# One attention stage of a four-layer block: mask addition and row maximum in one VectorE instruction per head instead of two over eight heads

## The chip, the cores and the metric

The kernel runs on one NeuronCore of a Trainium2 chip. The metric is the device time of one execution in microseconds, the median of several runs. The core has five engines with a queue each: PE (TensorE), DVE (VectorE), ACT (ScalarE), POOL (GpSimd) and SP (SyncE, which only issues DMAs). Each takes its instructions strictly in order; engines wait for each other by semaphores alone.

## The reference, cut to what matters

A stack of four gated layers over x of shape (16, 128, 256): in each, an attention block and a feed-forward block, each fed by a layer norm and added back with a tanh gate. The change is in the attention of layer 1, which has 32 heads of 8 elements:

```python
q, k, v = split_heads(h @ Wq), split_heads(h @ Wk), split_heads(h @ Wv)      # (16, 32, 128, 8), then rope on q and k
scores = einsum('bhqd,bhkd->bhqk', q, k) * inv_sqrt_d
scores = scores + attention_mask                                            # (16, 1, 128, 128), 0 or -1e9
scores = maximum(scores, finfo(float32).min)
w = softmax(scores, axis=-1)
attn = einsum('bhqk,bhkd->bhqd', w, v)
a_scores = tanh(gate) * softmax(einsum('bhqd,bhkd->bhqk', q, a_k) * inv_sqrt_d)  # second key set, from the context
attn = attn + einsum('bhqk,bhkd->bhqd', a_scores, a_v)
return attn @ Wo
```

## The kernel before, in words

Everything is written as queues by hand: for each engine a function lists its instructions, and marks (semaphores that count up) tie the queues together. `mark.at(n)` is the n-th increment of a mark.

The layer 1 attention works on 64 steps: step n is batch row b = n // 4 and the eight heads 8 * (n % 4) to 8 * (n % 4) + 7. All scores of a step are a 128 x 1024 tile in PSUM, 128 columns to a head. There are two score tiles with one buffer each: `self_bank` (banks 2 and 3) for the layer's own keys, `adapter_bank` (banks 4 and 5) for the keys from the context. For the own keys a step goes:

- PE, `pe_scores` (L1743): eight matmuls fill `self_bank`. For step n it first waits for `mask_used.at(n)`, the sign that step n - 1 has been read out of the bank.
- DVE, `dve_self_scores` (L1878 to L1888): one `tensor_tensor` over all 1024 columns adds the mask (broadcast over the heads) and writes the sum to `d_t[n % 3]` in SBUF (L1886, signals `mask_used`), then one `tensor_reduce` takes the maximum of each head, negated, into the eight columns of `max_t[n % 3]` (L1888, signals `maxed`). It waits for the sum by semaphore.
- The shift by the maximum is split: ACT, `act_shift` (L2003), does heads 0 to 3 with four activations (Identity with a bias per row), POOL, `pool_shift` (L2083), heads 4 to 7 with one `tensor_tensor`. Both wait for `maxed`.
- PE, `pe_turn` (L1764), transposes the eight 128 x 128 tiles into `turn_bank`, ACT exponentiates them (`act_exp`, L2011, two halves), PE, `pe_weigh` (L1789), multiplies with the values; DVE, `dve_normalise` (L1902 to L1907), reads the result, takes the reciprocal of the sums and scales, every second step; POOL, `pool_sums` (L2065), adds the two attentions.

For the context's keys `dve_adapter_max` (L1895) takes the negated maximum, which goes by a transposition on PE (`pe_turn_top`, L1732), ACT (L1986, L1987, L1991), POOL (`pool_rest_top` L2088, `pool_lo_top` L2092) and a DMA into the rows that `pe_adapter_turned` (L1775) reads.

The order is that of the loops over u in `pe_program`, `dve_program`, `act_program` and `pool_program`. At u DVE takes `dve_adapter_max(u + 5)`, then `dve_self_scores(u + 2)`, then a slot for the projections of a later pair of rows, `dve_turn_back` (L1914) and `dve_normalise(u - 1)`. PE takes `pe_turn(u)`, `pe_weigh(u - 1)`, `pe_adapter_turned(u)`, a projection slot, `pe_adapter_scores(u + 6)` (L1755) and `pe_scores(u + 3)`. ACT takes the exponents of u, and between its halves `act_shift(u + 1)`; POOL `pool_shift(u + 1)`, a slot, and `pool_sums` in every second step. Every eight steps (a pair of rows) the slots also hold the projections and rotations of a later pair: PE L1694, L1708, L1724, L1726 and L1797, DVE L1857 and L1859, ACT L1955 to L1978, POOL L2052, L2056, L2069, L2070 and L2078.

Of the kernel before, what the change touches and what calls it, by code (L numbers as in the profile page):

```python
# [11 lines left out]
ALU = mybir.AluOpType  # L12
ACT = mybir.ActivationFunctionType
AXX = mybir.AxisListType.X

P = 128
NB = 16
S = 128
# [9 lines left out]
LOWEST = -3.38e38  # L28
# [71 lines left out]
def split_cols(ap, k):  # L100
    return ap.rearrange("p (k n) -> p k n", k=k)
# [1499 lines left out]
def l1_attention(m):  # L1601
    nc, A = m.nc, m.A
    pe, dve, act, pool, sp = nc.tensor, nc.vector, nc.scalar, nc.gpsimd, nc.sync
# [8 lines left out]
    mask_t = [mem.f32(S) for _ in range(2)]  # L1612
    max_t = [mem.f32(8) for _ in range(3)]
# [4 lines left out]
    d_t = [mem.f32(8 * P) for _ in range(3)]  # L1618
# [21 lines left out]
    mask_ready, mask_used = m.mark("mask_ready"), m.mark("mask_used")  # L1640
# [9 lines left out]
    scored, maxed, shifted = m.mark("scored"), m.mark("maxed"), m.mark("diff_by_act")  # L1650
    shifted_pool = m.mark("sel_loaded")
# [17 lines left out]
    self_bank, adapter_bank = m.bank(2, 2), m.bank(4, 2)  # L1669
# [207 lines left out]

    def dve_self_scores(n):  # L1878
        b = n // 4
        d3, s3, mx = split_cols(d_t[n % 3], 8), split_cols(self_bank, 8), max_t[n % 3]  # L1880
        dve.wait_ge(*scored.at(n + 1))
        if n >= 3:
            dve.wait_ge(*turned.at(4 * (n - 3) + 2))
        if n % 4 == 0:
            dve.wait_ge(*mask_ready.at(b + 1))
        dve.tensor_tensor(d3, s3, mask_t[b % 2].unsqueeze(1).broadcast_to([P, 8, S]), ALU.add).then_inc(*mask_used.up())  # L1886
        dve.wait_ge(*mask_used.at(n + 1))
        dve.tensor_reduce(mx, d3, AXX, ALU.max, negate=True).then_inc(*maxed.up())  # L1888

    def dve_adapter_max(n):  # L1890
        b, s = divmod(n, 4)
# [39 lines left out]
    def dve_program():  # L1931
        dve.wait_ge(*m.x_l0f.at(NBLK))
        dve_norm_stats(1)
        dve.wait_ge(*v_cleared.now())
        for u in range(FIRST, LAST):
            if 0 <= u + AHEAD < NS:
                dve_adapter_max(u + AHEAD)
            if 0 <= u + 2 < NS:
                dve_self_scores(u + 2)
            dve_pro_slot(2 * u)  # L1940
            if u >= 3 and u % 2 and u <= NS + 1:
                dve_turn_back((u - 3) // 2)
            if 1 <= u <= NS:
                dve_normalise(u - 1)
            dve_pro_slot(2 * u + 1)
            dve_ffn_norms(u)
        dve_ffn_apply(7)
# [51 lines left out]
    def act_shift(n):  # L1999
        act.wait_ge(*maxed.at(n + 1))  # L2000
        for j in range(4):
            d = d_t[n % 3][:, j * P:(j + 1) * P]
            last = act.activation(d, d, ACT.Identity, bias=max_t[n % 3][:, j:j + 1])  # L2003
        last.then_inc(*shifted.up())

    def act_exp(i):
# [28 lines left out]
    def act_program():  # L2035
        act.wait_ge(*m.x_l0f.at(NBLK))
        act.wait_ge(*v_cleared.now())
        for u in range(FIRST, LAST):
            if 0 <= u < NS:
                act_exp(2 * u)  # L2040
            act_pro_slot(2 * u)
            if 0 <= u + 1 < NS:
                act_shift(u + 1)
            if 0 <= u < NS:
                act_exp(2 * u + 1)
            act_pro_slot(2 * u + 1)
# [32 lines left out]

    def pool_shift(n):  # L2080
        d3, mx = split_cols(d_t[n % 3][:, BANK:2 * BANK], 4), max_t[n % 3][:, 4:8]
        pool.wait_ge(*maxed.at(n + 1))
        pool.tensor_tensor(d3, d3, mx.unsqueeze(2).broadcast_to([P, 4, S]), ALU.add).then_inc(*shifted_pool.up())  # L2083

    def pool_rest_top(b):
        pool.wait_ge(*top_hi.at(b + 1))
# [45 lines left out]
    def pool_program():  # L2132
        pool.wait_ge(*m.x_l0f.at(NBLK))
        pool_roots(1)
        for kind in "aq":
            pool_clear_stack(kind, 2)
        for u in range(FIRST, LAST):
            if 0 <= u + 1 < NS:
                pool_shift(u + 1)
            pool_pro_slot(2 * u)  # L2140
            if 1 <= u <= NS and u % 2 == 0:
                pool_sums(u // 2 - 1)
            pool_pro_slot(2 * u + 1)
            for n in FFN_NORMS.get(u - NS, ()):
                ln_root(m, n, f_var, f_rstd)
# [2374 lines left out]
```

## Time and profile before

| | |
|---|---|
| median of 3 runs | 1979.42 us (1979.06 to 1988.81) |
| the profiled execution | 1980.39 us, of which the span of the program's instructions 1979.1 us |
| busy in the span | PE 87%, DVE 69%, ACT 48%, POOL 40% |
| mean granted clock of TensorE | 0.95 of full |
| first and last own-score sum (L1886) of the changed stage | 625.3 and 976.8 us |

The busy shares are means over all eight blocks. The changed stage lies between about 610 and 990 us, a fifth of the span; what a change in it is worth is read from the queues in that stretch. In the rows below a line of the timeline gives the start from the span's start, the length, the engine, the line of the kernel, the operation, what it writes and reads, its shape and how many were merged. The time from one start to the next on one engine is called the pitch here; it is shorter than the length where two instructions overlap.

### The profile page before, as it was taken

How to read it: one execution, taken by the hardware profiler on the slowest of the kernel's cores; microseconds unless marked ns; L12 is line 12 of the kernel's file. 1: busy time of each engine (PE TensorE's matmuls, PEld its weight loads, DVE VectorE, ACT ScalarE, POOL GpSimd, SP SyncE). 2: the span in 40 equal slices, each digit the busy share in tenths (PEclk: the TensorE clock that was granted, in tenths of full speed). 3: DMA queues.
4: the chain of work that ended last, by engine and by line, in shares of the span. 5: the costliest groups of instructions: out<-in, count | busy, mean ns of one | idle time of the engine just before them, and what ended most of it. 6: DMA issues, size and time to landing. Idle time of an engine off the chain costs nothing.

```text
span 1979.1 us, 35080 instructions
## 1 busy us (share of the span) xinstructions
PE 1716.5 (87%) x12221; PEld 1181.1 (60%) x12221; DVE 1370.8 (69%) x3299; ACT 942.1 (48%) x2227; POOL 789.6 (40%) x957
## 2 busy tenths in 40 slices
PE   6888888959897888888888787777999999987998
PEld 2444444636665777777666555455777777766445
DVE  8888873613357898988836889874576676666446
ACT  2666663203323676767735456433444444443352
POOL 3333321264654555655334555211124334433340
PEclk7999999979997999999989799789999999999899
DMA  4444422046863344334023453108200000030767
GB/s 108 104 120 102 94 55 79 31 161 225 298 178 84 79 86 85 78 78 89 16 82 96 120 148 87 42 1 275 78 18 36 32 8 4 13 96 13 232 214 305
DMA packets 180430, 200.35 MB, mean 101 GB/s; under 512 B 86500, under 2 KB 150129, under 8 KB 176928
## 3 DMA queue, kind: packets, MB, share of 16 engines
q1 hardware_dynamic: 161920, 155.92, 28.9%
q0 software_dynamic: 15168, 41.54, 6.1%
q8 instruction: 99, 1.62, 0.4%
q10 hardware_dynamic: 3168, 0.66, 0.2%
q14 instruction: 75, 0.61, 0.1%
HBM read 131.88 MB, written 75.44 MB: 105 GB/s over the span
## 4 chain that ended last, share of the span: by engine, by line
PE 49%; DVE 23%; ACT 8%; issue 8%; POOL 4%; DMA 3%; another core or an unknown queue 2%; ACTq 1%; SPq 1%; DVEq 0%; POOLq 0%
PE psum L3464 3%; PE psum L1052 3%; PE psum L3390 3%; PE psum L389 3%; PE psum L1329 2%; DVE sbuf L539 2%; PE psum L3439 2%; PE psum L352 2%; PE psum L3457 2%; PE psum L2276 2%; ACT sbuf L3827 2%; PE psum L1348 2%; PE psum L1064 2%; PE psum L4047 1%
## 5 line engine op out<-in xcount | busy, mean ns | idle before, releaser
L539 DVE TENSOR_REDUCE sbuf<-psum 128x2 f32<-128x512 f32 x256 | 164.9, 686 | 34.2 <-PE psum L352 33.2
L190 POOL TENSOR_TENSOR sbuf<-sbuf 128x1 f32<-128x1 f32 x128 | 73.2, 574 | 271.8 <-DVE sbuf L182 271.5
L2011 ACT ACTIVATE sbuf<-psum 128x512 f32<-128x512 f32 x256 | 138.6, 594 | 73.8 <-PE psum L1764 69.1
L3827 ACT ACTIVATE sbuf<-psum,sbuf 128x128 f32<-128x128 f32 x256 | 113.6, 456 | 89.0 <-DVE sbuf L3639 88.8
L681 ACT ACTIVATE sbuf<-psum 128x1024 f32<-128x1024 f32 x128 | 130.4, 1020 | 37.2 <-PE psum L374 29.7
L3919 POOL DMA_INDIRECT l_slot_inputs<-sbuf x96 | 97.2, 1013 | 100.7 <-DVE sbuf L3710 75.7
L3464 PE MATMUL psum<-sbuf 128*128 128x256 f32 x512 | 123.8, 385 | 4.9 <-DVE sbuf L3657 4.9
L3390 PE MATMUL psum<-sbuf 128*128 128x256 f32 x512 | 117.0, 382 | 0.8 <-ACT sbuf L3791 0.8
L352 PE MATMUL psum<-sbuf 112*128 112x256 bf16 x512 | 104.1, 288 | 12.8 <-DVE sbuf L539 7.7
L3390 PEld LDWEIGHTS psum<-sbuf 128*128 128x128 f32 x512 | 97.0, 192 | 20.6 <-issue 8.6
L3464 PEld LDWEIGHTS psum<-sbuf 128*128 128x128 f32 x512 | 93.5, 193 | 16.1 <-issue 5.8
L352 PEld LDWEIGHTS psum<-sbuf 112*128 112x128 bf16 x512 | 41.6, 101 | 91.2 <-DVE sbuf L539 52.9
L1895 DVE TENSOR_REDUCE sbuf<-psum 128x8 f32<-128x1024 f32 x64 | 77.5, 1211 | 26.2 <-PE psum L1755 26.2
L1052 PE MATMUL psum<-sbuf 128*128 128x512 f32 (+1 forms) x192 | 88.0, 602 | 0.0
L2003 ACT ACTIVATE sbuf<-sbuf 128x128 f32<-128x128 f32 x256 | 81.5, 398 | 0.0
L3597 DVE COPY sbuf<-psum 128x1024 f32<-128x1024 f32 x32 | 39.2, 1224 | 60.2 <-ACT sbuf L3798 40.1
L1888 DVE TENSOR_REDUCE sbuf<-sbuf 128x8 f32<-128x1024 f32 x64 | 78.1, 1220 | 2.2
L3835 ACT ACTIVATE sbuf<-psum 128x512 f32<-128x512 f32 x64 | 38.4, 600 | 85.0 <-PE psum L3447 84.6
L374 PE MATMUL psum<-sbuf 128*128 128x512 bf16 x256 | 78.1, 387 | 0.3 <-ACT sbuf L681 0.2
L1886 DVE TENSOR_TENSOR sbuf<-psum,sbuf 128x1024 f32<-128x1024 f32 x64 | 77.6, 1213 | 1.1 <-PE psum L1743 1.1
L1789 PE MATMUL psum<-sbuf 128*16 128x128 f32 x2048 | 70.5, 280 | 8.2 <-DVE sbuf L1902 6.9
L1764 PE MATMUL psum<-sbuf 128*128 128x128 f32 x512 | 71.7, 284 | 6.7 <-ACT sbuf L2011 6.6
(436 smaller groups left out, 4507.7 us busy)
## 6 DMA issues: line engine op xcount, KB each, us to landing
l_pair_outputs<-sbuf SPq DMA_DIRECT2D x24, 512.0 KB, 7.1
sbuf<-in_l_gu_pairs SPq DMA_DIRECT2D x32, 384.0 KB, 8.4
sbuf<-l_pair_outputs SPq DMA_DIRECT2D x16, 768.0 KB, 16.0
sbuf<-l_q_parts SPq DMA_DIRECT2D x16, 384.0 KB
l_q_parts<-sbuf SPq DMA_DIRECT2D x64, 96.0 KB, 2.3
sbuf<-l_q_parts SPq DMA_DIRECT2D x32, 192.0 KB
l_k_parts<-sbuf SPq DMA_DIRECT2D x64, 96.0 KB, 2.2
sbuf<-l_k_parts SPq DMA_DIRECT2D x32, 192.0 KB
```

Source lines behind the costliest of these rows:

```text
L352: last = pe.matmul(score_bank[v % 2][:, j * T0:(j + 1) * T0], q3[0:STACK + 48, h, c * P:(c + 1) * P], k3[0:STACK + 48, h // 4, :], start=T ...
L374: last = pe.matmul(shift_bank[u % 2][:, j * BANK:(j + 1) * BANK], k3[:, g, kc * P:(kc + 1) * P], q_stack[b % 3][:, lo:lo + BANK], start=Tr ...
L539: dve.tensor_reduce(top3[:, 2 * hp:2 * hp + 2, c], score_bank[v % 2].rearrange("p (j t) -> p j t", j=2), AXX, ALU.max, negate=True).then_i ...
L681: act.activation(e_t[u % 12], shift_bank[u % 2], ACT.Exp).then_inc(*exped.up())
L1052: last = pe.matmul(up_bank[v % 2][0:M, n * BANK:(n + 1) * BANK], wn[:, k, fs], xt_t[blk][:, k, :], start=(k == 0), stop=(k == KD - 1))
L1888: dve.tensor_reduce(mx, d3, AXX, ALU.max, negate=True).then_inc(*maxed.up())
L2003: last = act.activation(d, d, ACT.Identity, bias=max_t[n % 3][:, j:j + 1])
L2011: act.activation(e_t[i % 4][:, h * BANK:(h + 1) * BANK], turn_bank[:, h * BANK:(h + 1) * BANK], ACT.Exp).then_inc(*exped.up())
L3390: last = pe.matmul(q_bank[:, j * N:(j + 1) * N], w.wq[:, k, (4 * g + j) * P:(4 * g + j + 1) * P], xt_t[pair % 2][:, k, :], start=(k == 0), ...
L3464: last = pe.matmul(out_bank[:, 0:D], o_t[b % 2][:, h * P:(h + 1) * P], w.wo[:, h, :], start=(h == 0), stop=(h == H3 - 1))
L3827: last = act.activation(e_t[u % 3][:, j * P:(j + 1) * P], score_bank[:, j * P:(j + 1) * P], ACT.Exp, bias=mt[:, j:j + 1], scale=rq[:, lo + ...
L3919: pool.indirect_dma_start(out=route.x_slots[:, :], out_offset=bass.IndirectOffsetOnAxis(ap=route.slot[b][:, k:k + 1], axis=0), in_=xr_t[b ...
```

## The change

One fused instruction per head (`tensor_tensor_reduce`) replaces the sum over eight heads and the maximum over eight heads. It reads 128 columns of `self_bank` and the 128 x 128 mask, writes -(score + mask) to `d_t`, and the minimum of what it wrote, which is the negated maximum, to one column of `max_t`. The two shifts take the turned sign: ACT scales by -1 before it adds the bias, POOL subtracts the tile from the broadcast bias. The two marks change their meaning: `maxed` is now signalled after head 3, for ACT, and `mask_used` after head 7, for POOL and for `pe_scores`. One semaphore wait inside `dve_self_scores` is gone.

```diff
     def dve_self_scores(n):
         b = n // 4
-        d3, s3, mx = split_cols(d_t[n % 3], 8), split_cols(self_bank, 8), max_t[n % 3]
+        mask, mx = mask_t[b % 2], max_t[n % 3]
         dve.wait_ge(*scored.at(n + 1))
         if n >= 3:
             dve.wait_ge(*turned.at(4 * (n - 3) + 2))
         if n % 4 == 0:
             dve.wait_ge(*mask_ready.at(b + 1))
-        dve.tensor_tensor(d3, s3, mask_t[b % 2].unsqueeze(1).broadcast_to([P, 8, S]), ALU.add).then_inc(*mask_used.up())
-        dve.wait_ge(*mask_used.at(n + 1))
-        dve.tensor_reduce(mx, d3, AXX, ALU.max, negate=True).then_inc(*maxed.up())
+        for h in range(2):
+            for j in range(4 * h, 4 * h + 4):
+                head = slice(j * P, (j + 1) * P)
+                last = dve.tensor_tensor_reduce(d_t[n % 3][:, head], self_bank[:, head], mask, -1.0, -LOWEST, ALU.add, ALU.min, mx[:, j:j + 1])
+            last.then_inc(*(maxed, mask_used)[h].up())
...
     def act_shift(n):
-            last = act.activation(d, d, ACT.Identity, bias=max_t[n % 3][:, j:j + 1])
+            last = act.activation(d, d, ACT.Identity, bias=max_t[n % 3][:, j:j + 1], scale=-1.0)
...
     def pool_shift(n):
         d3, mx = split_cols(d_t[n % 3][:, BANK:2 * BANK], 4), max_t[n % 3][:, 4:8]
-        pool.wait_ge(*maxed.at(n + 1))
-        pool.tensor_tensor(d3, d3, mx.unsqueeze(2).broadcast_to([P, 4, S]), ALU.add).then_inc(*shifted_pool.up())
+        pool.wait_ge(*mask_used.at(n + 1))
+        pool.tensor_tensor(d3, mx.unsqueeze(2).broadcast_to([P, 4, S]), d3, ALU.subtract).then_inc(*shifted_pool.up())
```

## Rows read from the trace of the kernel before

**Rows 1.** Busy time by stretch: window, us, then each engine, clock, DMA.
```profile
core 0: us, PE busy (x) PEld busy (x) DVE busy (x) ACT busy (x) POOL busy (x), PEclk, DMA share, GB/s
650.00:950.00 300.00, 258.94 (x3623) 217.25 (x3621) 265.19 (x354) 209.12 (x525) 171.78 (x240) 0.98 0.38 82
```
**Rows 2.** Groups by line, of DVE: count | busy us, mean ns | idle before.
```profile
L1888 DVE TENSOR_REDUCE sbuf<-sbuf 128x8 f32<-128x1024 f32 x64 | 78.1, 1220 | 2.2
L1886 DVE TENSOR_TENSOR sbuf<-psum,sbuf 128x1024 f32<-128x1024 f32 x64 | 77.6, 1213 | 1.1 <-PE psum L1743 1.1
L1859 DVE TENSOR_TENSOR sbuf<-psum,sbuf 128x256 f32<-128x256 f32 x32 | 11.9, 415 | 0.0
L567 DVE TENSOR_TENSOR sbuf<-psum,sbuf 128x64 f32<-128x64 f32 x64 | 11.4, 220 | 1.1
```
**Rows 3.** Waits, 650 to 950 us: total us, times, longest us.
```profile
DVE sbuf L1895 <- PE psum L1755: 16.5, 15, 2.3
DVE sbuf L1902 <- PE psum L1789: 10.6, 9, 1.2
PE psum L1743 <- DVE sbuf L1886: 0.5, 1, 0.5
POOL sbuf L2065 <- DVE sbuf L1907: 75.1, 26, 7.1
```
**Rows 4.** Timeline of DVE, one and a half steps.
```profile
830.02 1.21 DVE L1886 TENSOR_TENSOR sbuf<-psum,sbuf 128x1024 f32<-128x1024 f32 x1
831.26 1.22 DVE L1888 TENSOR_REDUCE sbuf<-sbuf 128x8 f32<-128x1024 f32 x1
832.40 0.42 DVE L178 BATCH_NORM_STATS2 sbuf<-sbuf 128x6 f32<-128x256 f32 x1
...
833.07 0.15 DVE L182 TENSOR_SCALAR sbuf<-sbuf 128x1 f32<-128x1 f32 x1
833.14 0.42 DVE L178 BATCH_NORM_STATS2 sbuf<-sbuf 128x6 f32<-128x256 f32 x1
```
**Rows 5.** The chain that ended last, 829 to 852 us: start, us, what.
```profile
832.40 3.08 issue
835.48 0.02 POOLq L2087
...
837.78 1.26 ACT sbuf L2003 x4
...
849.71 1.80 PE psum L1694 x8
```
**Rows 6.** Timeline of DVE: short instructions without a wait between them.
```profile
61.29 0.36 DVE L567 TENSOR_TENSOR sbuf<-psum,sbuf 128x64 f32<-128x64 f32 x2
852.14 0.75 DVE L1859 TENSOR_TENSOR sbuf<-psum,sbuf 128x256 f32<-128x256 f32 x2
456.58 0.14 DVE L1385 COPY sbuf<-sbuf 128x1 f32<-128x1 f32 x1
456.64 0.14 DVE L1386 TENSOR_SCALAR sbuf<-sbuf 128x1 uint32<-128x1 f32 x1
```
**Rows 7.** Timeline of DVE: short instructions that wait for the one before.
```profile
382.86 0.29 DVE L1151 TENSOR_TENSOR sbuf<-sbuf 128x128 f32<-128x128 f32 x1
383.19 0.29 DVE L1153 TENSOR_REDUCE sbuf<-sbuf 128x8 f32<-128x128 f32 x1
```
**Rows 8.** Timeline of all engines around one step.
```profile
826.95 1.22 DVE L1888 TENSOR_REDUCE sbuf<-sbuf 128x8 f32<-128x1024 f32 x1
830.67 1.04 POOL L2083 TENSOR_TENSOR sbuf<-sbuf 128x512 f32<-128x512 f32 x1
830.67 1.28 ACT L2003 ACTIVATE sbuf<-sbuf 128x128 f32<-128x128 f32 x4
831.68 0.61 PE L1743 MATMUL psum<-sbuf 96*128 96x128 bf16 x8
832.58 1.12 PE L1764 MATMUL psum<-sbuf 128*128 128x128 f32 x8 [0.29 <-ACT sbuf L2011]
834.73 1.07 PE L1789 MATMUL psum<-sbuf 128*16 128x128 f32 x32 [1.03 <-DVE sbuf L1902]
835.51 0.59 POOL L2065 TENSOR_TENSOR sbuf<-sbuf 128x64 f32<-128x64 f32 x2 [3.11 <-DVE sbuf L1907]
```
**Rows 9.** Timeline of DVE at the stage's end.
```profile
964.73 1.21 DVE L1886 TENSOR_TENSOR sbuf<-psum,sbuf 128x1024 f32<-128x1024 f32 x1
968.58 1.22 DVE L1886 TENSOR_TENSOR sbuf<-psum,sbuf 128x1024 f32<-128x1024 f32 x1
971.79 1.18 DVE L1886 TENSOR_TENSOR sbuf<-psum,sbuf 128x1024 f32<-128x1024 f32 x1
```
**Rows 10.** All instructions of one line, whom they wait for, who waits for them.
```profile
L2083 POOL TENSOR_TENSOR sbuf<-sbuf x64: 1027/1036/1052, 629.9 to 983.3; 128x512 f32<-128x512 f32 x64
DVE sbuf L1888: 5.7, 4
```

## The prediction

> **What bounds the kernel now.** I read the groups by line first, to place the changed instructions: 64 sums and 64 maxima of 1.21 to 1.22 us each, 156 us of DVE in all, between 625 and 978 us [rows 2]. Then the busy time of that stretch alone: in 300 us from 650 us, DVE is busy 265.2 us (88%), PE 258.9 (86%), ACT 209 and POOL 172 [rows 1]. No engine but DVE and PE comes near its limit, and the two are close. The waits tell which of them leads. DVE stands still for PE some 27 us in these 300 (16.5 us before L1895, 10.6 us before L1902), while PE waits for the bank that DVE reads only once, 0.5 us [rows 3]. POOL waits 75 us for DVE's L1907, and what stands behind it in POOL's queue waits too. The chain of waits shows what that is worth: from 832.40 to 835.48 it has 3.08 us of "issue" on POOL [rows 5], and the timeline gives that gap its owner, `pool_sums` waiting 3.11 us for DVE L1907 [rows 8], behind which stand the small POOL steps that ACT and then PE wait for. So the piece is a DVE stretch in disguise, and one that starts with the two instructions of the change at 830.02 [rows 4]. After it the chain goes over ACT and PE [rows 5] for some 16 us, in which DVE, though full, is not what ends last. At the stage's end the sums follow each other by 3.85 and 3.21 us with DVE full in between [rows 9]: there every nanosecond of DVE counts.
>
> A step takes (976.8 - 625.3) / 63 = 5.58 us on average (first and last L1886 start). DVE's idle share, 34.8 us in 300, is 0.65 us of each step.
>
> **What the change removes.** The two instructions take, from the start of the sum to the start of the next instruction, 832.40 - 830.02 = 2.38 us [rows 4]. The second waits for the first, so its start is 1.24 us behind, a little more than the first's length; the next one, with no such wait, starts 1.14 us behind.
>
> **What it adds.** Eight instructions of 128 columns, one input in PSUM and one in SBUF. None like it is in the trace, so I build its cost from its relatives. Two sums of 256 columns from PSUM and SBUF take 0.75 us together, where one takes 0.415: the pitch is 0.33 us [rows 2, 6]. Two of 64 columns take 0.36 us, one of them 0.22: a pitch of 0.14 us [rows 2, 6]. The line through both is 1.0 ns per column, and gives 0.205 us at 128 columns. Then the minimum must be written out, one value per row. I take it as an instruction of its own, as small as the 128x1 ones of L1385 and L182: those start 0.06 to 0.07 us apart when nothing is waited for [rows 4, 6]. I take 0.065, so 0.27 us a head and 8 x 0.27 = 2.16 us a step: 0.22 us less than now. The even point is 2.38 / 8 = 0.298 us a head.
>
> The bounds: if the write-out were free, a head costs 0.205 and a step 1.64 us, 0.74 us less. If the write-out had to wait until the main instruction is through, the main's pitch is that of dependent instructions of this size, 383.19 - 382.86 = 0.33 us [rows 7], and with 0.065 a head costs 0.395, a step 3.16 us, 0.78 us more. I take the value near the middle because the rows without a wait are the nearer relatives: there is no semaphore between the eight instructions.
>
> The Trainium skill bears on this at two places. "Vector Engine (DVE) Microarchitecture Reference", section Measured stream behaviour on trn2, says that an instruction costs about 75 ns beyond its columns once the queue overlaps, programs of several micro-operations included. That would be 8 x (133 + 75) + 8 x 76 = 2.27 us for sixteen instructions, an estimate, and a saving of 0.11 us a step; the rows here are a little below it. Against the change speaks "VectorE: DVE Perf Modes", section on the TRN2 errata: a fixed price of 120 cycles for an instruction that reads PSUM and 58 for one that reads SBUF, and its advice is to have few, large instructions. By it the step would cost about 8 x 258 + 8 x 61 = 2.55 us, an estimate, 0.17 us more than now. The pitch of 0.33 us at 256 columns leaves 0.06 us of fixed price for a PSUM source [rows 6], so the trace disagrees with the larger figure.
>
> **What moves beside it.** `self_bank` was free 1.21 us after a step's start on DVE, now after all eight, 2.16 us: 0.95 us later. In rows 8, PE's L1743 starts at 831.68, and the sum that frees the bank ended at 831.23; it would now be free at about 832.2, 0.5 us later than PE took it. Behind it in PE's queue is L1764, which had 0.29 us of idle before it, and then L1789, which waited 1.03 us for DVE [rows 8]; the delay ends there. Price nothing, and if that cover were gone 0.5 us in perhaps three of eight steps, 64 x 3/8 x 0.5 = 12 us. ACT may start its shift after head 3, 1.1 us into the step instead of 2.4. But its four activations at 830.67 use the maximum of the step before, which ended at 828.17, 2.5 us earlier [rows 8]: ACT is held by its own queue, so nothing is gained. POOL waited for the maximum 4 times, 5.7 us in all [rows 10], and gets it 0.2 us sooner. The turned operands cost no more: the same shapes on both engines. The 128x512 shift on POOL stays at 1.04 us [rows 10]; I put both at zero with 0.1 us a step as a bound either way, since ACT and POOL are 70% and 57% busy [rows 1] and would hide it.
>
> **The sum.** 64 x 0.22 = 14 us less on DVE. Not all comes out: of the eight steps of a pair, the chain runs over two to four on DVE, the rest over ACT, POOL and PE; DVE's other time already has 0.65 us of idle a step, which would only grow. At the two ends of the stage nearly all comes out. I take half: 7 us. From the profiled execution's 1980.39 us that is 1973.4; the execution was 1.0 us above the median of 1979.42, so the forecast is 1972.4 us, 0.35% less.
>
> **Rivals.** (a) The write-out is hidden and the gain comes through. At 0.235 us a head a step saves 0.50 us, 32 us over the stage; half to two thirds is 16 to 21 us: 1958 to 1963 us. For it: the write-out reads no tensor, so the gap that rows 6 show between two instructions may shrink; DVE is the fullest engine. Against it: PE is 86% busy and would lead soon. Anything of over 0.27 us a step at a realised half gives more than 0.5%. (b) It gets slower, by one mechanism: main instruction and write-out do not overlap, at `dve_self_scores`, each head paying a pipeline's drain. From 0.298 us a head on DVE loses. At 0.395 a step is 0.78 us longer, 50 us over the stage; the idle 0.65 us a step takes up perhaps 0.3 of it, which leaves 30 us: 2010 us. At a milder 0.33 us a head it is 0.26 us, and 8 to 16 us: 1988 to 1995. For it: rows 7, and an instruction of a kind the trace doesn't hold. Against it: no row has an unforced drain. (c) The later release of the bank makes PE late and eats the gain: half of the 12 us above against the 7 gained, 1978 us. Against it: PE waited for this bank once in 300 us, and two waits stand behind it as cover. (d) The fused instruction might leave maximum or sum to be done twice: the diff shows neither remains, I give it nothing.
>
> **How the numbers follow.** The forecast 0.42, (a) 0.27, (b) 0.20, (c) 0.11. The range from 1958 to 1990 us holds the forecast and (c), most of (a) and the mild end of (b), and leaves out the serial case and a free write-out that comes through fully (1948 at two thirds of 47 us). 0.5% is 9.9 us, about what a measurement here can tell from no change. The forecast's own spread (0.25 to 0.29 us a head) reaches from 1967 to 1978, so a third of it counts as faster: 0.27 + 0.13 = 0.40 for faster; 0.40 for within 0.5% with (c) and the rest; 0.20 for slower.
>
> **What would show it.** The group of the fused instruction: 512 of them, with a mean of about 0.29 us and a pitch of head to head of 0.27 us with its write-out; if the pitch is above 0.30, (b). PE's wait before L1743 for DVE should appear in a few more steps by a few tenths; if it sums to over 10 us, (c). DVE's busy time in 650 to 950 us should fall and its waits for PE rise from 27 us; L2003 and L2083 should keep their durations. The forecast is wrong if the last score instruction of the stage doesn't start about 7 us sooner, or if the time changes outside 610 to 1000 us.

## The result

| | before | after |
|---|---|---|
| median, same chip, 5 runs each | 1982.45 us (1979.06 to 1988.81) | 1964.88 us (1964.35 to 1976.86) |
| ratio, 95% interval | | 0.9918 (0.9895 to 0.9941) |
| DVE for one step's scores, first start to next instruction | 2.38 us | 1.68 us |
| first to last start of PE's scores L1743 | 623.2 to 976.6 us | 622.9 to 961.4 us |

0.8% faster, 16 us, in the range forecast (1958 to 1990 us) and some 7 us below the forecast value. The forecast started from 1979.42 us, the median of three of the five runs of before in this table, so the ratio is the fairer comparison: 0.35% less was forecast, 0.8% less was measured.

The gain shows in the stage. In both kernels the first scores start at 623 us; the last start is 15.2 us sooner after the change, where the forecast had about 7:

```profile
L1743 PE MATMUL psum<-sbuf x512: 216/219/314, 622.9 to 961.4; 96*128 96x128 bf16 x171
```

(All instructions of a line: shortest/median/longest ns, then first and last start.) The profiled execution of the changed kernel took 1976.86 us all the same, the longest of its five. It lost the rest outside the changed stage: from the end of the stage's last PE matmul (L1797, 978.4 us) to the end it needed 997 us, where the trace of before needed 985. Another execution of the same program (`after_again`) needed 986 us, and the other kernels below between 981 and 992. That scatter belongs to the stages behind, which are the same code, and it goes with the clock granted to TensorE in them: 0.93 of full in those 997 us, 0.94 in the 985 us of before, 0.95 in the 986 us of `after_again`.

The same holds between whole executions. Beside `after_again` the kernel before ran 34 times, from 1983.55 us at a mean granted clock of 0.952 to 1999.67 us at 0.940. Over the runs of that series a clock lower by 0.01 goes with 11 to 13 us more (an estimate, by lines fitted to the recorded times and clocks). The gain itself is not the clock: the mean is 0.947 in the 34 runs of before and 0.947 in the 11 of the changed kernel.

### The profile page after: what moved, and what is told of

Read it like the earlier page. It is cut to its first block, busy times and chain, and to the rows that moved or that the text cites. A ratio compares the mean times of both kernels' runs of the same rounds, so it can differ in the third digit from the quotient of the medians.

```text
span 1975.5 us, 35976 instructions
## 1 busy us (share of the span) xinstructions
PE 1726.9 (87%) x12221; PEld 1186.7 (60%) x12221; DVE 1330.4 (67%) x4195; ACT 942.1 (48%) x2227; POOL 790.8 (40%) x957
## 4 chain that ended last, share of the span: by engine, by line
PE 51%; DVE 20%; ACT 10%; issue 7%; POOL 4%; DMA 3%; another core or an unknown queue 2%; ACTq 1%; SPq 1%; DVEq 0%; POOLq 0%
PE psum L3392 3%; PE psum L1052 3%; PE psum L389 3%; PE psum L3466 3%; PE psum L1329 2%; DVE sbuf L539 2%; PE psum L3441 2%; PE psum L352 2%; ACT sbuf L3829 2%; PE psum L3459 2%; PE psum L2278 2%; PE psum L1348 2%; PE psum L1064 2%; PE psum L1764 1%
## 5 line engine op out<-in xcount | busy, mean ns | idle before, releaser
L1889 DVE CUSTOM_DVE_ANT_0 sbuf<-psum,sbuf 128x128 f32<-128x128 f32 x512 | 112.5, 284 | 0.5 <-PE psum L1743 0.5
L3392 PEld LDWEIGHTS psum<-sbuf 128*128 128x128 f32 x512 | 98.7, 195 | 21.5 <-issue 8.8
L3466 PEld LDWEIGHTS psum<-sbuf 128*128 128x128 f32 x512 | 93.6, 193 | 16.1 <-issue 5.8
L2005 ACT ACTIVATE sbuf<-sbuf 128x128 f32<-128x128 f32 x256 | 81.4, 398 | 0.0
L3459 PE MATMUL psum<-sbuf 128*128 128x512 f32 x128 | 69.3, 623 | 9.8 <-ACT sbuf L3837 9.8
L3441 PEld LDWEIGHTS psum<-sbuf 128*128 128x128 f32 x512 | 65.8, 195 | 17.3 <-issue 15.1
L1764 PE MATMUL psum<-sbuf 128*128 128x128 f32 x512 | 70.5, 281 | 5.2 <-ACT sbuf L2013 5.0
```

The source lines that it names most:

```text
L1889: last = dve.tensor_tensor_reduce(d_t[n % 3][:, head], self_bank[:, head], mask, -1.0, -LOWEST, ALU.add, ALU.min, mx[:, j:j + 1])
L3392: last = pe.matmul(q_bank[:, j * N:(j + 1) * N], w.wq[:, k, (4 * g + j) * P:(4 * g + j + 1) * P], xt_t[pair % 2][:, k, :], start=(k == 0), ...
L3441: last = pe.matmul(score_bank[:, j * P:(j + 1) * P], q[:, 4 * g + j, i * P:(i + 1) * P], kT_t[b % 3][:, g * P:(g + 1) * P], start=True, st ...
L3459: pe.matmul(av_bank, v_t[b % 3][:, g * P:(g + 1) * P], eT_t[u % 2], start=True, stop=True).then_inc(*valued.up())
L3466: last = pe.matmul(out_bank[:, 0:D], o_t[b % 2][:, h * P:(h + 1) * P], w.wo[:, h, :], start=(h == 0), stop=(h == H3 - 1))
```

## The profile after

One head of the fused form is two instructions, as the timeline of DVE shows (start, us, engine, line):

```profile
828.59 0.28 DVE L1889 CUSTOM_DVE_ANT_0 sbuf<-psum,sbuf 128x128 f32<-128x128 f32 x1
828.80 0.08 DVE L1889 DVE_READ_ACCUMULATOR2_ANT sbuf<- 128x1 f32 x1
828.80 0.28 DVE L1889 CUSTOM_DVE_ANT_0 sbuf<-psum,sbuf 128x128 f32<-128x128 f32 x1
829.01 0.08 DVE L1889 DVE_READ_ACCUMULATOR2_ANT sbuf<- 128x1 f32 x1
829.01 0.30 DVE L1916 STREAM_TRANSPOSE sbuf<-sbuf 128x128 f32<-128x128 f32 x1
```

A head starts 0.21 us after the head before, and the read of the accumulator starts at the same 10 ns as the next head: it stands in the list, but not in the pitch. Eight heads take 1.68 us, so DVE saves 0.70 us a step, 45 us over the stage. The groups by line answer to [rows 2]:

```profile
L1889 DVE CUSTOM_DVE_ANT_0 sbuf<-psum,sbuf 128x128 f32<-128x128 f32 x512 | 112.5, 284 | 0.5 <-PE psum L1743 0.5
L1889 DVE DVE_READ_ACCUMULATOR2_ANT sbuf<- 128x1 f32 x512 | 42.2, 82 | 0.0
```

Busy time in the same 300 us as in [rows 1], from 650 to 950 us:

```profile
650.00:950.00 300.00, 269.08 (x3820) 227.61 (x3818) 241.56 (x1128) 219.78 (x554) 176.28 (x246) 0.98 0.38 81
```

PE rises from 86 to 90% and ACT from 70 to 73%: their work is unchanged and passes in less time; DVE falls from 88 to 81%, though it too passes more steps. The waits, which answer to [rows 3]:

```profile
DVE sbuf L1904 <- PE psum L1789: 23.2, 14, 2.6
DVE sbuf L1897 <- PE psum L1755: 22.7, 16, 3.9
DVE sbuf L1857 <- PE psum L1694: 9.4, 12, 1.5
```

DVE now waits for PE 55 us of 300 where it waited 31 (27 and a few at L1857). PE's wait for the score bank (L1743 for DVE) is under no row of that window; over the whole stage it is 2.6 us in 4 places, where before it was 3.4 us in 7. The chain that ended last, in the stretch that answers to [rows 5], has no fused instruction in it; DVE is on it only with the rotation (L1857, L1859):

```profile
824.62 1.70 issue
...
828.63 1.26 ACT sbuf L2005 x4
829.89 0.95 ACT sbuf L2013 x2
830.84 0.49 ACT sbuf L1957
831.33 0.04 issue
831.37 1.13 PE psum L1724 x4
832.50 0.86 PE psum L1726 x4
...
837.78 1.12 PE psum L1764 x8
838.90 1.00 PE psum L1789 x32
839.89 0.67 PE psum L1775 x8
840.56 1.80 PE psum L1694 x8
842.36 0.02 issue
842.38 0.53 DVE sbuf L1857
```

Before, the same chain had 3.08 us of disguised DVE time there ("issue", while POOL waited for DVE's L1907); now that piece is 1.70 us, in which POOL's L2067 waits 1.73 us for DVE's L1909. From ACT's shift to DVE's L1857 it is ACT and PE in turns, 13.75 us in both kernels (837.78 to 851.53 before, 828.63 to 842.38 after).

## The experiments

Each kernel ran against the kernel before on the same chip; the ratio is to it. The interval of a ratio reaches about 3 to 6 us to either side, and a length of the stage is that of one profiled execution at one granted clock. Theory A: the gain is DVE's shorter step, and as much of it comes out as DVE leads. Theory B: it comes from the early signal after head 3 and the wait that is gone.

**The changed kernel again** (no edit).

> The changed kernel once more, as the yardstick of this chip. Theory A (VectorE's shorter step is the whole gain: 1.69 us for the eight heads instead of 2.38, 44 us over 64 steps, of which about a third comes out): a ratio of 0.992 to the kernel before, some 1965 to 1967 us, and again a stage that ends 15 to 16 us sooner. Theory B (the gain is mostly that ScalarE may shift after head 3 and that one wait is gone): the same number here.

Measured: 0.9935 (0.9915 to 0.9956); last scores at 958.4 us, 18 us sooner than before. The result repeats in another series of runs, in which the kernel before took 1990.75 us.

**DVE's time given back.** Behind the fused instructions:

```diff
             last.then_inc(*(maxed, mask_used)[h].up())
+        if n:
+            dve.wait_ge(*padded.at(n))
+        dve.tensor_reduce(idle_t[:, 0:2], m.ident.unsqueeze(1).broadcast_to([P, 2, P]), AXX, ALU.max).then_inc(*padded.up())
```

> The changed kernel, with one idle VectorE maximum over 128x256 of a constant behind the eight fused instructions of each step: about 0.33 us more VectorE time a step (21 us in all), nothing else changed, the signals of the step not delayed. Theory A: half of VectorE's saving is gone, and the time rises by 4 to 9 us over the changed kernel, to 1969 to 1975. Theory B: no change, within 2 us of the changed kernel.

> The same with 128x640: about 0.73 us more VectorE time a step, so that a step costs VectorE as much as before the change (2.4 us) while ScalarE still gets its maxima early and the bank is free 0.5 us later than before. Theory A: back to the time of the kernel before, ratio 0.997 to 1.003. Theory B: stays below, at a ratio of 0.992 to 0.995.

> The changed kernel with an idle maximum over 128x384 behind each step's fused instructions: a VectorE step of about 2.15 us, between the 2.015 us that cost nothing (ratio 0.9927 against 0.9935) and the 2.415 us that cost the whole gain (0.9995). Theory A2 (there is a knee: up to about 2.0 us a step another loop sets the pace, above it over half of each VectorE microsecond comes out): ratio 0.995 to 0.997. Rival A1 (a straight line from 1.69 us on, the flat part being scatter): 0.9965 to 0.998 as well at this point, so the profile has to tell: A2 expects VectorE's waits for TensorE's L1755 and L1789 below 35 us in 650 to 950 us, and the stage some 5 us longer than with 128x256.

Measured, with DVE's time for a step as the traces have it, the waits of DVE for PE (three lines as above) in 650 to 950 us, the length of the stage from the first start of the scores to their last, and the clock granted in that stretch:

| DVE's step | kernel | ratio, 95% interval | DVE waits for PE | stage | clock |
|---|---|---|---|---|---|
| 1.68 us | changed | 0.9918 (0.9895 to 0.9941) | 55.3 us | 338.5 us | 0.97 |
| 1.68 us | changed, again | 0.9935 (0.9915 to 0.9956) | 52.7 us | 334.5 us | 0.98 |
| 2.015 us | idle 128x256 | 0.9927 (0.9901 to 0.9952) | 42.0 us | 343.1 us | 0.98 |
| 2.15 us | idle 128x384 | 0.9952 (0.9934 to 0.9969) | 38.1 us | 348.1 us | 0.98 |
| 2.415 us | idle 128x640 | 0.9995 (0.9976 to 1.0014) | 30.1 us | 357.1 us | 0.97 |
| 2.385 us | before | 1 | 30.6 us | 353.4 us | 0.97 |

The largest dose decides. With DVE's old time the whole gain is gone, to within about 4 us, though the early signal, the missing wait, the new bank release and the turned signs are all still there: theory B falls, theory A stands.

How the gain is spread is less sharp. By its ratio alone the first dose cost nothing, as theory B had it, and the point at 2.15 us came out as the knee theory (A2) had it: ratio 0.9952, 33.2 us of waits at L1755 and L1789, a stage 5 us longer than with 128x256. But a straight line fits the ratios within their intervals as well, and the stage in the traces rises through the first dose too, by 5 to 9 us. The runs' clocks can account for the flat piece: the twelve runs with 128x256 had a mean granted clock of 0.951, the kernel before and the changed one beside them 0.947. Compared at equal clock, by the line through the runs (an estimate, good to about 2 us each; it leaves aside that a kernel may itself shift the clock), the gain is 14 us for the changed kernel, 10 with 128x256, 6 with 128x384 and none with 128x640. That is about a third of the DVE time throughout. A flat stretch or a knee is not shown.

**The sum by head, the maximum over all.**

```diff
-        dve.tensor_tensor(d3, s3, mask_t[b % 2].unsqueeze(1).broadcast_to([P, 8, S]), ALU.add).then_inc(*mask_used.up())
+        for j in range(8):
+            head = slice(j * P, (j + 1) * P)
+            last = dve.tensor_tensor(d_t[n % 3][:, head], self_bank[:, head], mask_t[b % 2], ALU.add)
+        last.then_inc(*mask_used.up())
```

> The kernel before, with its one sum over 1024 columns cut into eight sums of 128 columns; the maximum stays one instruction over 1024. Measures the pitch of a plain 128-column sum from PSUM and SBUF. If the write-out of the fused instruction is hidden, the pitch here is the same 0.205 to 0.211 us as that of the fused instruction; if the fused one pays for it, it is shorter here. The step costs VectorE about 1.65 + 0.1 + 1.14 = 2.9 us, 0.5 us more than before. Theory A with VectorE near the bound: 15 to 30 us slower than before, 1995 to 2010. Rival C (TensorE sets the pace and VectorE only follows): under 5 us slower.

Measured: 1.0032 (1.0012 to 1.0052), a stage of 365.8 us, 12 us longer than before for 64 x 0.45 = 29 us more DVE. The timeline of DVE:

```profile
833.04 1.66 DVE L1888 TENSOR_TENSOR sbuf<-psum,sbuf 128x128 f32<-128x128 f32 x8
834.74 1.22 DVE L1891 TENSOR_REDUCE sbuf<-sbuf 128x8 f32<-128x1024 f32 x1
```

Eight plain sums take 1.66 us with the last one's full 0.28, a pitch of 0.198 us. The fused head's is 0.211: maximum and write-out together cost 13 ns a head. The time (0.3%, 6 us more) lies between what A expected (15 us and more) and what C expected (under 5 us), and misses both: of 29 us more DVE about a quarter comes out. So by the times of the runs the share is no larger with a longer DVE step than with a shorter one; by the stage alone it would be two fifths, at a clock of 0.96 against 0.97.

**The bank released late, in the kernel before.**

```diff
         if n:
-            pe.wait_ge(*mask_used.at(n))
+            pe.wait_ge(*maxed.at(n))
```

> The kernel before, except that TensorE's scores of the next step wait for the maximum (2.4 us into the step) instead of the sum (1.2 us): the bank is free 1.2 us later, VectorE's work unchanged. My step for the later release says that its delay is taken up behind it: under 3 us. The rival in which the bank holds TensorE up: 10 us or more slower, 1990 us and up, with waits of TensorE's L1743 for VectorE in most steps.

Measured: 0.9995 (0.9973 to 1.0018). PE did wait for it, and it cost nothing:

```profile
L1743 PE MATMUL psum<-sbuf x512: 216/219/314, 626.8 to 975.6; 96*128 96x128 bf16 x171
its engine sat idle before it (us, times) until:
  DVE sbuf L1888: 34.6, 49
```

PE stands still for 34.6 us before L1743, in 49 places, where the kernel before has 3.4 us. The stage took 349 us against 353, at a clock of 0.98 against 0.97. PE's idle time over the whole stage is the same, 48.0 us against 49.8: the waits moved to L1743 from the instructions behind it. In 650 to 950 us PE's wait for ACT before L1764 went from 4.9 to 1.2 us, that before L1724 from 8.8 to 5.4, and that before L1797 from 7.0 to 4.7.

**ScalarE's shift waits for all eight heads.**

```diff
     def act_shift(n):
-        act.wait_ge(*maxed.at(n + 1))
+        act.wait_ge(*mask_used.at(n + 1))
```

> The changed kernel, except that ScalarE's shift waits for all eight heads instead of the first four, 0.85 us later. Theory A: no difference to the changed kernel, within 2 us. Theory B (the early start of the shift brings the gain): 5 us or more of the gain go.

Measured: 0.9925 (0.9897 to 0.9953). No difference to the changed kernel is resolved; theory B's 5 us are at the edge of this interval. The profiled execution alone looks like B, with a stage of 343.9 us against 338.5 and 334.5, but its granted clock there was the lowest of the three (0.96 against 0.97 and 0.98). Over all runs, at equal clock, this kernel gains some 15 us and the changed one 14 (an estimate as above, to about 2 us each). So the early signal is worth little or nothing.

**The bank released in halves.**

```diff
-        if n:
-            pe.wait_ge(*mask_used.at(n))
         q3, k3 = stack["q"][b % 3], stack["k"][b % 2]
         for j in range(8):
+            if n and j % 4 == 0:
+                pe.wait_ge(*(maxed, mask_used)[j // 4].at(n))
```

> The changed kernel, except that TensorE takes the two banks of the scores one by one: the first four matmuls of a step wait for heads 0 to 3 of the step before (0.85 us into it), the last four for heads 4 to 7. A possible better version. If the bank holds TensorE up in the changed kernel, 2 to 6 us faster than it; if not (no wait of L1743 for VectorE is seen in 650 to 950 us of its trace), the same within 2 us. I expect the same.

Measured: 0.9928 (0.9902 to 0.9953), a stage of 338.1 us. The same, as expected.

**Using the room on DVE.** Three versions that take shifts off ACT.

```diff
# dve_shift2; dve_shift4 the same with all four heads
-        for j in range(4):
+        for j in range(2):                                  # act_shift
...
+        dve.wait_ge(*maxed.at(n + 1))
+        d3 = split_cols(d_t[n % 3][:, 2 * P:4 * P], 2)
+        dve.tensor_tensor(d3, mx[:, 2:4].unsqueeze(2).broadcast_to([P, 2, S]), d3, ALU.subtract).then_inc(*shifted_dve.up())
# dve_shift2_one_input
+        for j in (2, 3):
+            d = d_t[n % 3][:, j * P:(j + 1) * P]
+            last = dve.tensor_scalar(d, d, mx[:, j:j + 1], None, ALU.subtract, ALU.min, accum_out=idle_t[:, j:j + 1])
```

> The changed kernel, with the shift of heads 2 and 3 moved from ScalarE (two activations, 0.63 us a step) to VectorE (one subtraction over 128x256, about 0.33 us a step, the dose that cost nothing as an idle one). Theory A2 says that VectorE has this room, and that the loop which sets the pace now runs over ScalarE's shifts and exponents and TensorE (ScalarE L2005 and L2013 are over a fifth of its chain in the stage): 5 to 12 us faster than the changed kernel, ratio 0.987 to 0.990. Rival A1 (VectorE still leads): the same or 2 to 7 us slower than the changed kernel.

> The same with all four of ScalarE's heads moved to VectorE (128x512, about 0.6 us a step, ScalarE 1.26 us less). VectorE's step is then 2.3 us, nearly what it was before the change. Theory A2: VectorE leads again, ratio 0.990 to 0.997, worse than with two heads. Rival D (ScalarE's time was the bound of the changed kernel): better than with two heads, below 0.987.

> As the version with heads 2 and 3 shifted on VectorE, but by one instruction per head that reads a single tensor from SBUF and the maximum as a scalar, and also writes out an accumulator nobody reads (heads 2 and 3 keep the plain sign). In the earlier version the shift read two tensors from SBUF; it took 0.41 to 0.42 us where no GpSimd instruction ran and 0.7 to 2.8 us where one did (mean 0.79). Theory E: two SBUF inputs wait for GpSimd's instruction, one does not; then the two shifts take about 0.5 us together, always, and the time is below the earlier version's: ratio 0.989 to 0.993. Rival F (any VectorE instruction on SBUF beside GpSimd is stretched): the shifts reach 0.5 us each and more, ratio 0.994 or above.

Measured: two heads 0.9945 (0.9928 to 0.9962), four heads 1.0032 (1.0012 to 1.0052), two heads with one input 0.9902 (0.9874 to 0.9930). The first two miss what A2 expected (0.987 to 0.990, and 0.990 to 0.997), and rival D (below 0.987) is out by far. They don't test A2 cleanly: the shift was meant to take 0.33 us a step for two heads and 0.6 for four, and its rows took 0.79 and 1.06 us on average. All instructions of the two-head shift (shortest/median/longest ns), then the longest one in the timeline beside POOL:

```profile
L1896 DVE TENSOR_TENSOR sbuf<-sbuf x64: 414/616/2794, 626.9 to 972.6; 128x256 f32<-128x256 f32 x64
```

```profile
811.03 1.03 POOL L2091 TENSOR_TENSOR sbuf<-sbuf 128x512 f32<-128x512 f32 x1
...
811.62 2.79 DVE L1896 TENSOR_TENSOR sbuf<-sbuf 128x256 f32<-128x256 f32 x1
812.03 0.42 POOL L2100 TENSOR_TENSOR sbuf<-sbuf 32x128 bf16<-32x128 f32 x1
812.41 0.72 POOL L2108 TENSOR_TENSOR sbuf<-sbuf 128x256 f32<-128x256 f32 x1
813.11 1.03 POOL L2091 TENSOR_TENSOR sbuf<-sbuf 128x512 f32<-128x512 f32 x1
814.34 0.30 DVE L1922 STREAM_TRANSPOSE sbuf<-sbuf 128x128 f32<-128x128 f32 x1
```

POOL has four instructions back to back from 811.03 to 814.14, and DVE's ends 0.27 us after the last. With one SBUF tensor to read and the maximum as a scalar, beside the same POOL work, the length never moves:

```profile
L1901 DVE TENSOR_SCALAR_CACHE_REDUCE sbuf<-sbuf x128: 340/344/348, 628.1 to 972.2; 128x128 f32<-128x128 f32 x128
```

Theory E is borne out for the durations (the version also changes the operation and its size, which was not separated from the count of inputs). For the time, the two versions' intervals hardly overlap (0.9928 to 0.9962 against 0.9874 to 0.9930): one input is likely the better by some 0.4%, as E expects. They ran in different series, though, and the one-input runs had a mean clock of 0.953 where before had 0.948 beside them, so a part of it may be the clock. That it beats the changed kernel is not shown; DVE's step is 2.2 us in it, and ACT waits 80 us for PE's transposes in 650 to 950 us where it waited 62.

**Five heads on GpSimd.** `act_shift` does heads 0 to 2, `pool_shift` heads 3 to 7; the first half of `pe_turn` waits for both.

> The changed kernel, with head 3's shift moved from ScalarE to GpSimd, which then does five heads in one subtraction (about 1.29 us instead of 1.04; ScalarE 0.32 us less a step). VectorE is left alone. Theory A2 (ScalarE's shifts stand on the chain of the changed kernel): 2 to 6 us faster than the changed kernel, ratio 0.989 to 0.991. Rival G (GpSimd's queue stands on it as well, and the first transposes now wait for GpSimd too): the same or slower, 0.993 or above.

Measured: 0.9908 (0.9880 to 0.9936), a stage of 332.7 us against 334.5 and 338.5. The ratio lies where A2 expected it (0.989 to 0.991), but its interval holds both the changed kernel's ratios and the start of rival G's range (0.993). A hair better on every count and not resolved on any; POOL's 128x640 took 1.25 us. Which loop leads in the changed kernel stays open.

## Why the prediction was right, point by point

The direction, the engine and the price of what moves beside it were right. The size was not: 7 us forecast, 16 measured, and the last score instruction started 15.2 us sooner where the prediction had made about 7 its sign. That the time still lies in the range is owed to the range's width, and to two errors that work against each other: the saving on DVE was three times what I reckoned, and a smaller share of it came out.

- **What bounds the kernel**: right. DVE led, and only in part; giving its time back took the whole gain away.
- **What is removed, 2.38 us**: right.
- **The 128-column instruction, pitch 0.205 us, by a line through 64 and 256 columns**: right, 0.198 us for the plain sum.
- **The write-out, 0.065 us a head**: the term that was mis-sized. I took it as "an instruction of its own, as small as the 128x1 ones". It is one, 82 ns long, but it starts together with the next head; with the running minimum it costs 13 ns. I had no row of such a read, and took the nearest small instructions for it. The saving was therefore 0.70 us a step, not 0.22, close to the bound that I had named for a free write-out (0.74). The rows of L1385 and L182 are instructions that read SBUF; this one reads no tensor. Rival (a) named that as the reason; the hiding came true, more fully than it assumed, and the reason itself was not tested. Its 16 to 21 us hold the measured gain partly by luck: it reckoned half to two thirds of 32 us, where a third of 45 came out. By the Trainium skill's "Vector Engine (DVE) Microarchitecture Reference", section Measured stream behaviour on trn2, an instruction costs 1.04 ns a column and about 75 ns beyond its columns. The trace agrees for the fused instruction: 128 columns by the page are 0.133 us, and the measured pitch leaves 0.211 - 0.133 = 0.078 us. But that is paid once for the two instructions of a head, not twice as I had reckoned with the page.
- **Half of DVE's saving comes out**: too high, about a third did (16 of 45 us). The rest is in the waits: DVE's idle time for PE grew from 31 to 55 us in 300. The half was a guess between the two to four steps of eight on the chain and the stage's ends; no experiment shows which of these was too high. Whether the share depends on how much is taken is not resolved: a third with the saving given back in doses, a quarter with 29 us added.
- **The later bank costs nothing**: right, by the late and the half release. The few more waits that I expected before L1743 didn't come (2.6 us after, 3.4 before), since the step on DVE is 1.68 us and not 2.16. The cover was larger than I said, and not only before L1789: in the late release PE stood still 34.6 us before L1743 for free.
- **The early maximum for ACT and the turned signs cost and bring nothing**: right as far as the runs resolve it; L2005 and L2085 kept 0.39 and 1.04 us.
- **A slip in the rivals**: "over 0.27 us a step at a realised half gives more than 0.5%" should be 0.31 (9.9 / 32). The forecast doesn't hang on it.
- **Slower by unoverlapped write-outs** (b): excluded by the timeline.

## What to carry to other kernels

In this kernel each of the eight pieces of a large VectorE instruction cost only about 65 ns beyond its columns when no semaphore stands between them (a pitch of 0.198 us at 128 columns and 0.33 at 256, so 1.03 ns a column), and an accumulator written out per piece is nearly free: two passes over the same 1024 columns became one plus 0.6 us of fixed costs. A saving on the fullest engine comes out only in the share in which it leads, here about a third, with PE at 86% when DVE was at 88%. An idle instruction put back in several doses measures this share directly, and tells a saving in work from a saving in signals. Before small differences of such a series are read, the granted clock of the runs has to be looked at: here a difference of 0.004 seems to have hidden the price of the first dose.

## What the runs showed of the hardware that I had not expected

- The accumulator read of VectorE (82 ns in its row) starts with the next fused instruction and is over before that one ends: pitch 211 ns with it, 198 ns for a plain sum of the same shape without.
- A VectorE instruction with two fp32 inputs from SBUF stretched from 0.414 to 2.79 us beside GpSimd instructions on SBUF; one with a single SBUF input kept 0.340 to 0.348 us there, and the fused one (PSUM and SBUF) stayed at 0.244 to 0.290. The Trainium skill's "SBUF — State Buffer", section Who interferes with whom, has the rule: a VectorE instruction with two SBUF inputs contends with a GpSimd instruction that reads SBUF, over a port pair that works as an exclusive lock. The trace agrees with it, and shows more than the length of one GpSimd instruction: VectorE's ended only behind the fourth in a row.
- 34.6 us of TensorE waits on one line left TensorE's idle time in the stage at 48.0 us, where it was 49.8: idle time in front of an instruction is no loss where what follows would wait anyway.
- Executions of one and the same kernel differed by 16 us with the granted clock: 1983.55 us at 0.952, 1999.67 us at 0.940.
